# A two-layer relational graph attention kernel: the first stage rebuilt (doubled codes, run gathers without a copy, transform in half blocks, masks on ScalarE)

## The reference

```
xr    = einsum('nd,rdf->rnf', x, W)           # one transform per edge type
alpha = leaky_relu(xr[type,dst] @ q + xr[type,src] @ k, 0.2)
a     = softmax of alpha over the edges of one dst
out   = segment_sum(a * xr[type,src], dst) + b
```

## Time and profile before

| | us |
|---|---|
| median of 3 runs | 1432.45 (1432.42 to 1434.45) |
| the profiled execution | 1434.1 |
| its span in the profile | 1432.3 |
| granted TensorE clock, mean over the span | 0.951 |
| busy: PE, DVE, ScalarE | 1313.6, 1140.8, 730.8 |

### The profile page before, as it was taken

How to read it: one execution, slowest core, us unless ns; L and a number is a source line. 1 busy time by engine, 2 the same in 40 slices (tenths; PEclk the granted TensorE clock), 3 DMA queues, 4 the chain that set the end, 5 groups by cost and what they waited for, 6 DMA issues and landing times.

```text
span 1432.3 us, 20253 instructions
## 1 busy us (share of the span) xinstructions
PE 1313.6 (92%) x7162; PEld 1181.4 (82%) x7162; DVE 1140.8 (80%) x1875; ACT 730.8 (51%) x1243; POOL 6.5 (0%) x19
## 2 busy tenths in 40 slices
PE   1899999999944799999999999999997999999995
PEld 1798655555632799999999999999987999999995
DVE  2776999999597899898998998686954666866874
ACT  1542332111000899799898995325734445465462
POOL 1000000000000000000000000000000000000000
PEclk9885999999975799999999999999998999999997
DMA  6440001211101433233333322694457776578561
GB/s 198 164 174 0 34 34 47 108 56 53 48 22 41 142 123 102 78 113 94 97 98 94 94 57 84 218 310 145 164 207 272 230 256 211 188 225 274 172 212 42
DMA packets 85084, 189.01 MB, mean 132 GB/s; under 512 B 7659, under 2 KB 59362, under 8 KB 84998
## 3 DMA queue, kind: packets, MB, share of 16 engines
q1 hardware_dynamic: 84806, 187.39, 39.4%
q0 software_dynamic: 192, 0.45, 0.1%
HBM read 148.21 MB, written 41.53 MB: 132 GB/s over the span
## 4 chain that ended last, share of the span: by engine, by line
PE 77%; DVE 13%; DMA 4%; ACT 3%; issue 2%; SPq 0%; DVEq 0%; ACTq 0%; POOL 0%; POOLq 0%
PE ps L1085 22%; PE ps L1030 21%; PE ps L882 14%; PE ps L911 8%; PE ps L928 4%; DVE arena L1218 4%; PE ps L867 2%; DVE arena L1278 2%; PE ps L858 2%; DVE arena L1282 1%; ACT arena L665 1%; DMA arena<-in_L_gnn_W 1%; ACT arena L666 1%; DVE ps L1348 1%; PE ps L845 1%
## 5 line engine op out<-in xcount | busy, mean ns | idle before, releaser
L1030 PE MATMUL ps<-arena 128*128 128x193 f32 x2400 | 398.7, 328 | 1.7 <-DVE arena L1282 1.5
L1030 PEld LDWEIGHTS ps<-arena 128*128 128x128 f32 x2400 | 394.1, 191 | 4.3 <-DVE arena L1282 3.5
L882 PE MATMUL ps<-arena,xT 128*128 128x384 f32 x720 | 243.8, 489 | 0.0
L665 ACT ACTIVATE arena<-arena,misc 128x640 f32<-128x640 f32 x240 | 196.9, 820 | 41.8 <-DVE arena L1278 23.5
L882 PEld LDWEIGHTS ps<-arena,xT 128*128 128x128 f32 x720 | 133.0, 191 | 79.8 <-issue 0.6
L666 ACT ACTIVATE arena<-arena,misc 128x640 f32<-128x640 f32 x240 | 195.5, 815 | 0.0
L1278 DVE TENSOR_TENSOR arena<-arena 128x1280 f32<-128x1280 f32 x120 | 178.3, 1486 | 19.6 <-ACT arena L666 17.1
L1282 DVE SCALAR_TENSOR_TENSOR arena<-arena,Ct 128x1280 f32<-128x1280 f32 x120 | 179.0, 1492 | 14.5 <-DVE arena L1278 9.9
L1085 PE MATMUL ps<-g_hi,x2a 128*128 128x416 f32 (+1 forms) x540 | 155.5, 357 | 11.0 <-DVE g_lo L1435 9.6
L1218 DVE SCALAR_TENSOR_TENSOR arena<-arena,misc 128x1250 f32<-128x1250 bf16 x108 | 156.6, 1514 | 0.0
L1085 PE MATMUL ps<-g_hi,x2b 128*128 128x416 f32 (+1 forms) x540 | 152.4, 352 | 0.0
(11 more groups left out here) (176 smaller groups left out, 1602.2 us busy)
## 6 DMA issues: line engine op xcount, KB each, us to landing
x2a<-xr_d SPq DMA_DIRECT2D x41, 768.0 KB, 4.6
x2b<-xr_d SPq DMA_DIRECT2D x41, 768.0 KB, 4.4
arena<-xr_d SPq DMA_DIRECT2D x120, 193.0 KB, 2.4
xr_d<-stg SPq DMA_DIRECT2D x60, 384.0 KB, 3.1
arena<-ab_d SPq DMA_DIRECT2D x12, 1280.0 KB, 6.4
arena<-in_L_gnn_W SPq DMA_DIRECT2D x6, 2304.0 KB, 9.1
xr_d<-arena SPq DMA_DIRECT2D x30, 386.0 KB, 2.7
arena<-in_L_gnn_W SPq DMA_DIRECT2D x6, 1152.0 KB, 6.3
```

Source lines behind the costliest of these rows:

```text
L665: nc.scalar.activation(e1[t % 5][:, h, :], abr[:, r, h, :], ACT.Exp, bias=qk1t[:, t, col + R * H:col + R * H + 1])
L882: last = mm(ps[2 + 2 * (t % 2) + b][:, 0:HF], xT[:, kt, t * P:(t + 1) * P], weights(WOFF[1] + r)[:, kt, b * HF:(b + 1) * HF], start=kt == ...
L1030: last = mm(bank1(g, i)[:, o:o + HD + 1], e1[t % 5][:, h, i * P:(i + 1) * P], xring[t % NX][:, o:o + HD + 1], start=False, stop=True, skip ...
```

## The change

What it does, part by part:

- **Runs without a copy.** `runs_d` and its DMA are gone. GpSimd gathers the 160 runs from `code_d` at single elements. SP issues all of x right behind the writes of the codes, without waiting for the gathers. EP, the partitions of the edge arrays, is 80 in place of 125 (rows of 250 codes in place of 320). The transposes of the runs stand behind those of the eighth tile of x.
- **Doubled codes.** `slo` and `mcode` are kept as bf16, each value twice side by side (`slo_2`, `mcode_2`), in the order of the pairs. A pair is built with two TENSOR_TENSORs, of 768 and of 1440 elements, all operands bf16. Four copies make the doubled codes where one made `slo_w`.
- **Another order of the weights' work.** Four blocks' transposes and two products are done before the flag, the other 14 at intervals of two to three pairs (`WT_AT`, `WQ_AT`), and PE waits for the flag ahead of the pairs.
- **Transform in half blocks, logits ride.** The unit of the transform is one tile and one half (384 columns) of a type: 60 units, 4 PSUM banks, 4 staging buffers, 60 stores. The first half of type 0 has the 24 columns of `wqk1` behind it, in a buffer of its own (`w_b0`), so its ten units give the logits too; the logit matmuls and their copies are gone. From pair 34 on the 60 k-steps of these ten units are spread over the pairs (`steps0`).
- **Masks on ScalarE.** `mask1` writes `2e30 * count - 1e30` as bf16, 4 buffers; DVE takes the minimum with k where it added.
- **Maxima chain among the units.** The transposes of the maxima (4 banks) stand between given units (`MK_U`), the reduces of type r - 1 within `maxima(r)` from the fourth tile on, ab's transposes ahead of unit 57. ScalarE's order of evacuations and masks is sorted by estimated times (`UNIT_T`, `TILE_T`).
- **Second stage.** The order of its buffers in memory is `xring`, `e2`, `e1`; the waits of `xt_upper` follow it. The load of b1 is behind the last store, and DVE waits for it in the first `rows1`.

The diff, cut to its core:

```diff
-    EP = 125
+    EP = 80
+    UNITS1 = [(b, t) for b in range(2 * R) for t in range(NT)]
-    runs_d = nc.dram_tensor("runs_d", [NROW, RUNL], F32).ap()
...
+        slo_2 = edi.bitcast(BF16).rearrange("p (n a) -> p n a", a=2)
+        mcode_2 = u0.bitcast(BF16).rearrange("p (n a) -> p n a", a=2)
+        w_b0 = cut(B0_AT, KT * (HF + QC)).rearrange("p (k c) -> p k c", k=KT)
+        wqk1 = w_b0[:, :, HF:HF + QC]
+        NCN = 4
+        NS1 = 4
+        xring = [take(XB) for _ in range(NX)]
+        e2 = [take(2 * DH).rearrange("p (h d) -> p h d", h=2) for _ in range(2)]
         e1 = [take(2 * DH).rearrange("p (h d) -> p h d", h=2) for _ in range(5)]
+        e1 = [e1[-1]] + e1[:-1]
...
+        PRE = 4
+        WT_AT = {(i - PRE) * 7 // 3: i for i in range(PRE, R * KT)}
+        WQ_AT = {p + 2: i for p, i in WT_AT.items()}
+        WQ_AT.update({i: PRE - 2 + i for i in range(2)})
+        T_AT = max(WT_AT) + 4
+        NK0 = NT * KT
+        def steps0(pair):
+            n = PAIRS - T_AT
+            return range(max(0, NK0 * (pair - T_AT) // n), max(0, NK0 * (pair + 1 - T_AT) // n))
+        MASK_LAG, UNIT_T, TILE_T = 2, 42, 66
+        MK_U = [{28: (0, 2), 29: (2, 4), 32: (4, 6), 34: (6, 8), 35: (8, 10)},
+                {42: (0, 2), 43: (2, 4), 47: (4, 6), 49: (6, 8), 51: (8, 10)},
+                {54: (0, 4), 55: (4, 7), 56: (7, 10)}]
+        MKB = (6, 7, 0, 1)
+        RED_AT = 3
+        AB1_AT = 57
...
@@ sync
-            sp.wait_ge(S["code_out"], 32)
-            every = bass.AP(code_d.tensor, 0, [[GRAN, NROW], [1, RUNL]])
-            sp.dma_start(runs_d[:, :], every).then_inc(S["runs_out"], 16)
-            sp.wait_ge(S["rows_in"], 32)
-            sp.wait_ge(S["runs_in"], 32)
...
+            for u, (b, t) in enumerate(UNITS1):
+                if u == AB1_AT:
+                    ab_store(L1)
+                    for r in range(R):
+                        load_ab1(0, r)
...
+                    for i in range(NX):
+                        sp.dma_start(xring[i], xr_d[i, 0]).then_inc(xr_in[i], 16)
+                sp.wait_ge(S["t_evac"], u + 1)
+                sp.dma_start(xr_d[b // 2 * NT + t, b % 2], stg1[u % NS1]).then_inc(xr_out[u % NS1], 16)
@@ gpsimd
-            pool.wait_ge(S["runs_out"], 16)
-                nc.gpsimd.indirect_dma_start(runb[0:SW, s, :], None, runs_d[:, :],
+                nc.gpsimd.indirect_dma_start(runb[0:SW, s, :], None, code_d.rearrange("(e a) -> e a", a=1),
@@ scalar
+            def transform_out(u):
+                b, t = UNITS1[u]
+                act.wait_ge(S["t_done"], u + 1)
+                if u >= NS1:
+                    act.wait_ge(xr_out[u % NS1], 16 * (u // NS1))
+                if b == 0:
+                    nc.scalar.activation(qk1t[:, t, :], v[:, HF:HF + QC], copy)
+                    nc.scalar.activation(ks1[:, t, :], v[:, HF + QC // 2:HF + QC], copy, scale=SLOPE).then_inc(S["qk_ready"], 1)
+                nc.scalar.activation(o, v[:, 0:HF].rearrange("p (h c) -> p h c", h=2), copy).then_inc(S["t_evac"], 1)
+            def mask1(i):
+                if i >= NCN:
+                    act.wait_ge(S["mk_step"], (i - NCN + 1) * H)
+                nc.scalar.activation(cneg[i % NCN], Ct[:, i, :], copy, bias=-BIG, scale=2 * BIG).then_inc(S["mk_cneg"], 1)
+            events = [((u - NT + 1) * UNIT_T, 0, u) for u in range(NT, U1)] + [(max(0, i - MASK_LAG) * TILE_T, 1, i) for i in range(RS)]
+            for _, kind, i in sorted(events):
+                if kind == 0 and i == AB1_AT:
+                    ab_rows(L1)
+                (mask1 if kind else transform_out)(i)
@@ tensor
+            def unit1_step(u, kt):
+                b, t = UNITS1[u]
...
+                w = HF + QC if b == 0 else HF
+                v = w_b0[:, kt, :] if b == 0 else weights(R + b // 2)[:, kt, b % 2 * HF:(b % 2 + 1) * HF]
+                last = mm(unit1_bank(u)[:, 0:w], xT[:, kt, t * P:(t + 1) * P], v, start=kt == 0, stop=kt == KT - 1)
+            for i in range(PRE):
+                wt_transposes(i)
+                if i >= 2:
+                    wq_product(i - 2)
+            pe.wait_ge(S["flag_sum"], 1)
...
+            for u in range(NT, U1):
+                for r in range(R):
+                    for t in range(*MK_U[r].get(u, (0, 0))):
+                        mk_transpose(r, t)
+                if u == AB1_AT:
+                    ab_transposes(L1)
+                for kt in range(KT):
+                    unit1_step(u, kt)
@@ vector
-                        w = slo_w[:, bass.ds(s * SW + j * 4 + h * 2, 2), :]
-                        V.tensor_tensor(oh_s[:, h * 2 * RUN:(h + 1) * 2 * RUN, :].rearrange("p (c t) s -> p c t s", c=2),
-                                        i_s[:, :].unsqueeze(1).unsqueeze(1).broadcast_to([P, 2, RUN, P]),
-                                        w.unsqueeze(3).broadcast_to([P, 2, RUN, P]), ALU.is_equal)
-                        for c in range(2):
-                            for t in range(RUN):
-                                col = s * (RUN * SW) + j * 4 + (t * SW + h * 2 + c)
-                                last = V.tensor_scalar(ohm[(h * 2 + c) * RUN + t], i_m[:, :], mcode[:, bass.ds(col, 1)], None, ALU.is_equal)
+                        col = s * (RUN * SW) + j * (4 * RUN) + h * (2 * RUN)
+                        for o, w, iota, codes in ((oh_s, P, i_s, slo_2), (ohm_s, WM, i_m, mcode_2)):
+                            last = V.tensor_tensor(o[:, h * 2 * RUN:(h + 1) * 2 * RUN, :].rearrange("p n (b a) -> p n b a", a=2),
+                                                   iota[:, :].rearrange("p (b a) -> p b a", a=2).unsqueeze(1).broadcast_to([P, 2 * RUN, w // 2, 2]),
+                                                   codes[:, bass.ds(col, 2 * RUN), :].unsqueeze(2).broadcast_to([P, 2 * RUN, w // 2, 2]), ALU.is_equal)
...
-                    V.tensor_scalar(cneg[i % 2], Ct[:, i, :], 0.0, -BIG, ALU.is_equal, ALU.mult).then_inc(S["mk_cneg"], 1)
-                            last = V.scalar_tensor_tensor(m[:, h, 0:N], cneg[i % 2][:, 0:N], k, m[:, h, 0:N], ALU.add, ALU.max)
+                            last = V.scalar_tensor_tensor(m[:, h, 0:N], cneg[i % NCN][:, 0:N], k, m[:, h, 0:N], ALU.min, ALU.max)
+                    if r and RED_AT <= t < RED_AT + NT // 2:
+                        for s in range(2):
+                            reduce1(r - 1, 2 * (t - RED_AT) + s)
```

More of the change, by code:

```diff
@@ L281, in rgat @@
         w_in = [sem(f"w_in{i}") for i in range(2)]
-        xr_out = [sem(f"xr_out{i}") for i in range(2)]
+        xr_out = [sem(f"xr_out{i}") for i in range(NS1)]
         xr_in = [sem(f"xr_in{i}") for i in range(NX)]
@@ L618, in _ @@
                 last.then_inc(S["c_ready"], 1)
[L619 to L627 removed]
+                if pair - 1 in WT_AT:
+                    wt_out(WT_AT[pair - 1])
+                if pair - 1 in WQ_AT:
+                    wq_out(WQ_AT[pair - 1])
+                for n in steps0(pair - 1):
+                    if n % KT == KT - 1:
+                        transform_out(n // KT)
             def ab_rows(lay):
@@ L659, in _ @@
                     for t in range(NT):
+                        if g == 0 and r == 0 and t == 1:
+                            act.wait_ge(S["t_done"], U1)
                         step = g * RS + r * NT + t
@@ L912, in unit @@
                 last.then_inc(S["t_done"], 1)
+            for i in range(PRE):
+                wt_transposes(i)
+                if i >= 2:
+                    wq_product(i - 2)
+            pe.wait_ge(S["xt_ready"], NB_X)
             pe.wait_ge(S["flag_sum"], 1)
-            mm(ps[7][0:1, 0:1], small[:, 8:9], onesf[:, 0:1], start=True, stop=True).then_inc(S["flag_tot"], 1)
+            mm(ps[1][0:1, 0:1], small[:, 8:9], onesf[:, 0:1], start=True, stop=True).then_inc(S["flag_tot"], 1)
             pe.sem_inc(S["c_done"], 2)
-            pe.wait_ge(S["xt_ready"], NB_X)
+            pe.wait_ge(S["flag_ready"], 1)
             for pair in range(PAIRS):
@@ L974, in mk2_transpose @@
                 last.then_inc(S["mk2_tr"], 1)
-            def mk_transposes(u):
-                for t in range(NT):
-                    mk_transpose(u, t)
             def ab_transposes(lay):
@@ L1258, in _ @@
             dve.wait_ge(S["c_ready"], NW // 2 + 2)
-            dve.wait_ge(S["qk_ready"], 1)
-            maxima(0)
-            maxima(1)
-            for t in range(NT):
-                reduce1(0, t)
-            maxima(2)
+            dve.sem_inc(S["ct_final"], 1)
+            for r in range(R):
+                maxima(r)
             for t in range(NT):
```

306 lines of the change are left out of this document (130 added, 176 removed).

## The result

| | before | after |
|---|---|---|
| median of the runs, us | 1432.43 (4 runs, 1430.88 to 1434.45) | 1358.59 (4 runs, 1356.26 to 1360.28) |
| profiled execution / its span, us | 1434.1 / 1432.3 | 1356.26 / 1354.5 |
| ratio | | 0.9476, 95% interval 0.9463 to 0.9489 |
| first build of a pair, start | 45.53 | 40.12 |
| last copy of counts, end | 233.60 | 183.96 |

The kernel is 74 us faster where 94 were forecast. Nearly the whole difference stands in one stretch: the first 34 pairs last 74.9 us in place of 53.9.

A forecast was written before the change was run, and what follows sets the result against it. The chain of waits ends on TensorE nearly everywhere, so the second stage's first matmul decides: 381.7 instead of 476.6 us. 1434.1 - 94.9 + 0.5 = 1339.7 for the profiled execution, 1338 from the median, stated 1339; range 1327 to 1362.

The forecast's parts named there:

- the prediction's own last line: Whole forecast: wrong if the build is not halved, or the second stage starts after 395 us.
- D: Rival: ScalarE's fixed order or transposes hold PE, each tile of the maxima again at 6.25; +12, 1351 us; chance 0.08.
- C: Rival at the start: bulk loads delay the small gathers, pairs start at 46.5; +6, 1345 us; chance 0.07.
- The start of the pairs: Preparation before the pairs: first build at 40.5 us instead of 45.5, bounds 38.5 and 46.
- The build: DVE's one-hots of a pair: half width, 0.48 + 0.82 = 1.30 us, bounds 0.75 and 2.42.
- rival A: DVE's build stays at full width, 2.42 us a pair, and bounds the pairs; +75, 1414 us; chance 0.10.
- rival B: Re-reading one word of doubled codes slows DVE's packed form, 1.86 us a pair; +31, 1370 us; chance 0.05.
- the 80 pairs on PE: Counting pairs: 53.9 us for pairs 0 to 33, 69.5 for 34 to 79, together 123.4 against 187.4, at full clock.
- rival E: PE's clock stays low through the pairs, all prices there double; +114, 1453 us, slower than before; chance 0.03.
- Pairs 34 to 79, maxima, units, tail: Pairs 34 on to second stage: 69.5 us of pairs, last maximum 343.7, first second-stage matmul 381.7 instead of 476.6.
- Later stages: From the second stage on: reordered buffers make the third tile's upper part up to 1.9 us late; 0.5 us taken.
- the likeliest case's own range: Whole kernel: forecast 1339 us with its own range 1330 to 1350; chance 0.67.

The follow-up runs named there:

- e4: Changed kernel with each code kept once in f32, the same two TENSOR_TENSORs a pair; 1414.58 us, ratio 0.9879 to the kernel before.
- e1: Changed kernel with ScalarE copying a block's transposed weights in the pair that transposes them, not one pair later; 1349.32 us, ratio 0.9424 to the kernel before.
- f1: Changed kernel with that early copy of transposed weights plus 11 and 9 zero matmuls on PE before and behind the flag's matmul; 1337.62 us.
- f4: Changed kernel with x issued behind the gathers in two parts, as before, and runs transposed ahead of x's second part; 1365.33 us.
- f3: Changed kernel with the masks back on DVE, add in place of min; 1369.69 us, ratio 0.9567 to the kernel before.
- g1: Changed kernel with the earlier build: one 768 TENSOR_TENSOR with f32 codes and six TENSOR_SCALARs of 240 a pair; 1384.69 us.
- g2: Changed kernel with the early copy of transposed weights and 11 zero matmuls only ahead of the flag's matmul; 1346.11 us.

## Why the prediction was right where it was, and wrong in one step

By the prediction's own last line it is right on one count and wrong on the other: the build is halved, but the second stage starts at 402.55, after 395. That the time still lies inside the stated range is luck of a wide range. Its upper end of 1362 was tied to no mechanism; the dearest rivals inside it, D (1351) and C (1345), did not come at their prices, and the 19.6 us between 1339 and 1358.6 have another cause.

**The start of the pairs** held as a sum: 40.12 against 40.5. Its parts did not, and here too luck helped. The runs came sooner (DVE's cast at 27.55, not 29.8), and the doubling copies cost more: four of 3.57 us together, where I gave four 1.8. Two errors of opposite sign, of 2.3 and 1.8 us.

**The build** held exactly: 556 and 901 ns against 0.56 and 0.90, and DVE waits for PE. This was the step that rival A (e4: 1414.6) priced and rival B halved. B is refuted by L1188's mean alone: reading one doubled word over and over adds nothing to the half-width price. The Trainium skill's page "Vector Engine (DVE) Microarchitecture Reference", section 5.2, grants the full rate only to runs of at least two adjacent 4-byte words; the trace does not show that for a repeated word in packed form, and the measurement decides.

**The failed step** is "the 80 pairs on PE": "so I add 4.5 (first build, cold clock, waits): 53.9" and "I expect the full clock". Pairs 0 to 33 took 74.9 us, 21.0 more. The traced executions of e1 and f1 split them:
- 11.6 us (74.9 to 63.3, e1) is the late copy in thinly set pairs. The copy of the transposed weights stands behind the next pair's evacuation, and PE has nothing else to do between two counts. For waits I had 4.5, after the 51.5 - 45.9 = 5.6 us that the old first pairs lost. At the full clock seven pairs lose 12.18 - 10.74 = 1.4 us, so the 34 pairs under 7; the rest is the clock that fell with the waits.
- 7.7 us (63.3 to 55.6, f1 against e1) is the low clock of the first 16 us, set off by PE's waits of 3.37 and 2.32 us ahead of the first counts. It was in the 4.5 by name, "cold clock", and far too small: in the old pairs, from which the 4.5 was taken, the low clock lasted some 3 us.
- 1.7 us is what is left of f1 against 53.9. PE's waits for DVE in f1's pairs sum to 2.3 us, at five places, and the sum prices the 14 sets of transposes at 0.61 where its own row has 0.65, which is 0.6 us.

With both causes away the time is 1337.6 (forecast 1339). The two together are firm: 19.3 us of the traced pairs, 21.0 by the medians. How they split is not, since the traced executions of the changed kernel and of e1 (1345.98) are the fastest of their four, and e1's lie 6.2 us apart. By the medians the copy is worth 9.3 us and the start 11.7. What let me go wrong is the sentence that the new mix has the parts of the old one. It has, but it spreads them thinly, and so has waits the old one lacked (5.2 us for the copy, 0.2 there). The earlier trace rows also held the warning that I used only for rival E: 0.52 in the stretch from 97 to 133.5, where PE was 35.71 of 36.5 us busy. Rival E was the right mechanism at about a tenth of its 114 us: 7.7, and the nearly 5 that are left of the 11.6 when the 7 are taken off.

**Rival C** was there, but off the chain. With x issued first, the gathers land 6.1 us after their issue in the median, against 3.6 in f4, and the first one's result reaches DVE at 17.14, against 13.48. The pairs didn't start later for it, since PE was held by the load of x until 22.08 and takes the runs behind the eighth tile.

**Rival D** was half right too: ScalarE's fixed order does hold PE, yet in the pairs and not in the maxima, where I had looked (PE waits 1.84 us there, 1 forecast).

**Pairs 34 to 79, maxima, units, tail.** From the first matmul of 408 columns to the end of the last copy of counts 68.9 us against 68.1 (94.4 to 162.5); from the end of the counts to the first matmul of the second stage 218.6 against 219.2; first maximum 3.05 us behind the counts against 3.7. The masks' price, 12.3 us of DVE, came back as 11.1 in f3; the two engines meet within 2 us, so little of it was hidden.

**Later stages**: 3.8 us less where I had 0.5 more. From 402.55 the stretch takes 951.9 us against 955.7. No run followed this up. The second stage has 0.3 of it, the second layer's units 0.9, the third stage 2.5. In the traces of all twelve kernels with the change the stretch takes 951.2 to 954.5 us, though almost nothing differs there, so much of the 3.8 may be the spread of single executions.

Sum: 1339.7 + 20.85 (start of the second stage at 402.55, not 381.7) - 4.3 = 1356.2, the profiled execution. The median of 1358.6 lies above the likeliest case's own range, which ended at 1350.

**Where the 74 us come from**, by undoing one part at a time: doubled codes 26.1 (g1), masks on ScalarE 11.1 (f3), early x 6.7 (f4), later stages 3.8. The remaining 26 us or so I put down to the logit columns riding in the transform (before, 36.5 us at the low clock), the maxima chain among the units and the copy; these weren't undone separately, and parts undone singly need not add up.

## What to carry to other kernels

When small matmuls ride between steps of another engine, write down for every one the engine that hands it its operand and what stands ahead of that hand-over in its queue; a copy that sits one step too late cost 9.3 us here, more than its own waits, because the clock fell with them. Price a stretch of small matmuls at both clock levels, and a low stretch by how long it lasts in a trace, not by the wait that set it off: 3.05 us of waiting cost the old pairs some 3 us at the low clock, 2.32 us cost g2's pairs 16. And undo causes in pairs before you judge them: alone they gave 9.3 and 5.2 us, together 21.0.
